# Two operations moved earlier and two moved later in the tail of an RWKV and mixture-of-experts kernel

## What is computed

```python
x = layernorm(x + attn(x))      # mixes, key/value/receptance products, a recurrence over tokens, product with Wo
x = layernorm(x + ffn(x))

def ffn(x):                     # E = 8 experts, K = 2 taken, I = 16
    weights = softmax(x @ router_w.T)
    gate    = weights * topk_mask(weights, 2)
    h       = einsum('bth,eih->beti', x, down_w)
    a       = silu(h)
    return sum over experts of gate * (a @ up_w)
```

## Time and profile before

| | us |
|---|---|
| median of 3 executions | 460.04 |
| lowest and highest | 459.71, 460.34 |
| the profiled execution, its own time | 459.98 |
| its span in the profile | 458.2 |
| TensorE busy in the span | 444.6 (97%) |
| VectorE busy | 404.1 (88%) |
| ScalarE busy | 356.0 (78%) |
| GpSimd busy | 312.0 (68%) |

### The profile page before, as it was taken

How to read it: one execution, slowest core, us unless ns; L and a number is a source line. 1 busy time by engine, 2 the same in 40 slices (tenths; PEclk the granted TensorE clock), 3 DMA queues, 4 the chain that set the end, 5 groups by cost and what they waited for, 6 DMA issues and landing times.

```text
span 458.2 us, 6679 instructions
## 1 busy us (share of the span) xinstructions
PE 444.6 (97%) x1984; PEld 340.2 (74%) x1984; DVE 404.1 (88%) x616; ACT 356.0 (78%) x801; POOL 312.0 (68%) x300
## 2 busy tenths in 40 slices
PE   8999999999999999999999999999999999999993
PEld 3444567777888888888888888888888888888761
DVE  5989989899788989999898998989898996876976
ACT  1666757877888779888788888888798887768695
POOL 2355677588658998579858797569966694744334
PEclk9999999999999999999999999999999999999998
DMA  8703230033000042002320042100520022300016
GB/s 239 223 0 117 93 92 1 1 115 93 1 1 0 2 160 92 24 0 74 135 70 0 1 139 93 46 0 24 162 93 1 1 69 94 137 1 0 0 49 229
DMA packets 20244, 30.64 MB, mean 67 GB/s; under 512 B 2032, under 2 KB 7152, under 8 KB 20208
## 3 DMA queue, kind: packets, MB, share of 16 engines
q1 hardware_dynamic: 20208, 30.21, 20.3%
HBM read 21.82 MB, written 8.39 MB: 66 GB/s over the span
## 4 chain that ended last, share of the span: by engine, by line
PE 78%; DVE 5%; ACT 2%; POOL 2%; issue 1%; ACTq 0%; DVEq 0%
PE PH L449 5%; PE PV L330 5%; PE PV L336 5%; PE PV L331 5%; PE PR L336 5%; PE PR L330 5%; PE PK L330 5%; PE PR L331 5%; PE PK L336 5%; PE PK L331 5%; PE PP L359 4%; PE PP L360 4%; PE PP L364 4%; PE PT L431 3%; PE PP L379 2%
## 5 line engine op out<-in xcount | busy, mean ns | idle before, releaser
L592 ACT ACTIVATE PR<-PR 128x512 f32<-128x512 f32 x128 | 74.6, 583 | 29.8 <-PE PR L336 10.6
L1213 POOL TENSOR_TENSOR DQ<-DEN,EX 128x512 f32<-128x512 f32 x32 | 41.3, 1290 | 20.6 <-DVE DEN L871 20.6
L1219 POOL TENSOR_SCALAR NM<-SUM,RS 128x1 f32<-128x1 f32 x30 | 8.0, 267 | 62.1 <-ACT RS L592 62.1
L330 PE MATMUL PK<-KH,WKH 128*128 128x512 f32 x112 | 46.2, 413 | 0.6 <-DVE NUM L888 0.6
L925 DVE SCALAR_TENSOR_TENSOR KT<-D,VEC,XT 128x512 f32<-128x512 f32 x57 | 45.8, 851 | 0.0
L330 PE MATMUL PV<-VH,WVH 128*128 128x512 f32 x112 | 45.6, 407 | 0.0
L336 PE MATMUL PR<-RL,WRH 128*128 128x512 f32 x112 | 44.0, 393 | 0.7 <-POOL RL L1181 0.7
L330 PE MATMUL PR<-RH,WRH 128*128 128x512 f32 x112 | 44.5, 398 | 0.2 <-DVE RW L912 0.2
L336 PE MATMUL PV<-VL,WVH 128*128 128x512 f32 x112 | 43.9, 392 | 0.0
L336 PE MATMUL PK<-KL,WKH 128*128 128x512 f32 x112 | 43.9, 392 | 0.0
L331 PE MATMUL PK<-KH,WKL 128*128 128x512 f32 x112 | 43.8, 391 | 0.0
(11 more groups left out here) (275 smaller groups left out, 1285.7 us busy)
## 6 DMA issues: line engine op xcount, KB each, us to landing
XT<-in_xt SPq DMA_DIRECT2D x32, 256.0 KB, 3.3
XN<-in_x SPq DMA_DIRECT2D x28, 256.0 KB, 2.7
out<-XN SPq DMA_DIRECT2D x28, 256.0 KB, 2.0
X1T<-in_wo SPq DMA_DIRECT2D x1, 1024.0 KB, 5.1
XT<-in_x SPq DMA_DIRECT2D x4, 256.0 KB, 4.2
out<-XT SPq DMA_DIRECT2D x4, 256.0 KB, 2.4
X1T<-in_wk SPq DMA_DIRECT2D x2, 256.0 KB, 4.9
XN<-in_wv SPq DMA_DIRECT2D x2, 256.0 KB, 5.7
```

What stands on the lines that cost most here:

```text
L330: eng.matmul(dst[:, :], wh[:, c, o], high[:, c, :], start=(c == 0), stop=False)
L592: eng.activation(*a, **k).then_inc(q[s], 1)
L1213: eng.tensor_tensor(DQ[:, :], DEN[:, 0:T], EX[:, 1, :], ALU.add).then_inc(q["e"], 1)
```

## The change

Three orders in the tail are altered. No instruction is added or taken away, and no wait is altered.

```diff
@@ TensorE @@
             hidden(t7 + 2)
+            hidden(t7 + 3)
             ffn_up(t5 + 3)
-            hidden(t7 + 3)
             ffn_up(t6)
@@ ScalarE @@
             hidden_copy(t7 + 2)
-            spread2(t5 + 1)
             hidden_copy(t7 + 3)
             ffn_in(LAST + 1)
             ffn_out(LAST)
+            spread2(t5 + 1)
             spread2(t5 + 2)
             ffn_out(LAST + 1)
@@ VectorE @@
             silu(LAST)
-            residual2(t5 + 3)
             gate_scores(LAST + 1)
             gate_top(LAST + 1)
+            residual2(t5 + 3)
             silu(LAST + 1)
```

## The result

| | before | after |
|---|---|---|
| median, same chip, 21 executions each (us) | 460.05 | 460.87 |
| the profiled execution, its own time | 459.98 | 460.70 |
| its span | 458.2 | 458.9 |

The changed kernel takes 0.82 us more; the ratio is 1.002, with a 95% interval from 1.0014 to 1.0025. The forecast was 460.8. Of all executions reported here one stands apart and is left out of its comparison: one of the eleven of e1 took 1162.12 us, and as it was the profiled one, the same kernel was profiled once more as e5, in a single execution of 461.21 us.

What follows compares the result with a forecast made beforehand. Taken to bound the tail: ScalarE's full queue from the last score copy, through GpSimd's scalings to the piled-up stores. TensorE 0, VectorE's 0.50 hidden beside ScalarE's 0.80: 459.98 + 0.80 = 460.78, median 460.8 us, range 460.2 to 461.4.

Steps and rivals of the forecast that it cites:

- Starts at 441.26 again: gain 0: TensorE: tile 31's reordered down product waits for ScalarE's copy of the transposed tile, so gains 0, at most 0.14 us.
- Hidden, just: TensorE: running tile 23's up product later costs at most 0.95 us, absorbed by the wait before part 8's transposes.
- 0.90 less a credit of 0.10: ScalarE: tile 21's squares, moved into the full queue, make it 0.90 us late, less 0.10: a shift of 0.80.
- The credit of 0.10: VectorE's subtraction for the last scores: 0.10 us shorter once GpSimd no longer scales tile 21 beside it; bounds 0 and 0.10.
- + 0.50: VectorE: tile 23's residual, exposed before the last two multiplications, delays them 0.60 less 0.10 us; bounds 0.46 and 0.60.
- Side by side, and the larger counts: Tail: VectorE's 0.50 us and ScalarE's 0.80 us delays run in parallel to the end; only the larger counts.
- a sign of being wrong: End of kernel: the last store is issued 0.8 us later but the end moves by less.
- 0.80 for the whole: Final stores: their transfers pile up; the pile begins 0.80 us later, so the whole kernel ends 0.80 later.
- No loss: Rival, chance 0.17: the store queue hides ScalarE's delay, or only VectorE's 0.50 us shows; 460.0 to 460.5 us.
- The stores bunch: Rival, chance 0.12: stores from tile 21's on run into each other, adding one tile of 0.75 us; 461.5 at worst.
- The clock: Rival, chance 0.02: TensorE's idle time halves its clock, adding 7.7 us on nine tiles' up products; some 468 us.
- A gain: Rival, chance 0.03: the last score copy comes earlier, by at most 0.14 and 0.10 us; 459.8 us.

Runs made afterwards that it cites:

- e1: Kernel before with only ScalarE's squares of tile 21 moved behind the copy of part 7: 460.91 us against 459.98, ratio 1.0021.
- e5: Same kernel as e1, profiled once more in a single execution: 461.21 us.
- e6: Changed kernel with ScalarE's copy of tile 31's transposed form put ahead of part 7's activations: 460.65 us against 460.05 for the kernel before, ratio 1.0015.
- e3: Kernel before with only tile 31's down product put ahead of tile 23's up product on TensorE: 460.87 us against 459.98, ratio 1.0021.
- e2: Kernel before with only VectorE's residual of tile 23 moved between the last gate and its two multiplications: 460.62 us against 459.98, ratio 1.0013.
- e4: Kernel before with the diffs of e2 and e3 together, without ScalarE's move: 460.56 us against 459.98, ratio 1.0012.
- e7: Kernel before with squares of tiles 22 and 23 taken as a pair ahead of part 8's copy on ScalarE: 459.70 us against 460.05, ratio 0.9993.
- e8: e7's pair, plus tile 27's up product ahead of part 8's transposes and tile 29's variance on ScalarE: 459.40 us against 460.05 before, ratio 0.9987.

## Why the prediction was right

**TensorE.** "Starts at 441.26 again: gain 0" held to 0.01, and e6 showed that its reason held: with the copy out of the way the product starts 0.85 earlier. "Hidden, just" was a bound from long steps; really TensorE reached the transposes of part 8 with 0.25 to spare. What the prediction left unsaid is that the move alone is not free. With the residual in its old place it costs 0.89 (e3).

**ScalarE.** 0.90 less a credit of 0.10 was right in the whole and in each part: two pitches of 1.09, the wait swallowed, the copy at 446.95 in after and in e5. That this queue carries the loss is shown by e5, where VectorE is early and the loss is all there.

**The credit of 0.10.** The subtraction takes 0.17 when GpSimd's scaling is not beside it (after, e5) and 0.27 when it is (before, e2), and then it ends 0.02 behind that scaling: 443.25 and 443.23 before, 443.56 and 443.54 in e2. The Trainium skill ("SBUF — State Buffer", section "SBUF: two separate sides") states that a VectorE operation with two SBUF inputs and a GpSimd operation that reads SBUF exclude each other for a whole instruction. These ends agree with it. The credit is most of the 0.12 between the 0.80 and the 0.92 of the prediction.

**VectorE.** + 0.50 was forecast, 0.48 measured in the changed kernel, 0.57 in e2 where the credit is missing (0.60 forecast as the upper bound). Behind the last multiplication stand eight residuals, tiles 24 to 31, and not the seven of the prediction; nothing in its sum used the count.

**The sum.** "Side by side, and the larger counts" is what e1, e2 and e4 say: 0.93, 0.64, 0.58, and 0.82 for all. The store of tile 31 missed its place, however: 455.80 was said, 455.87 + 0.08 = 455.95 came. GpSimd's scaling of tiles 28 and 30 took 1.92 and not the 1.68 of the earlier trace rows, and VectorE's of tiles 29 and 31 took 1.26 for 1.48. The prediction had carried both durations over, though their overlap moves with 0.50 against 0.80. The end did not follow the 0.15. The prediction had named as a sign of being wrong that the last store is issued 0.8 later and the end moves by less: the store moved by 0.95 and the end by 0.80, so the sign came half true, against the last tile and not against the pile. The table has what tells the two apart, in the profiled executions: how much later than before, the shift of each profile taken off, tile 26's store is issued (the pile's beginning), the last store is issued, and the whole execution ends.

| | tile 26's store | last store | end |
|---|---|---|---|
| after | 0.79 | 0.95 | 0.80 |
| e2 | 0.56 | 0.56 | 0.56 |
| e3 | 0.87 | 0.87 | 0.87 |
| e4 | 0.57 | 0.57 | 0.57 |
| e5 | 0.79 | 0.96 | 0.98 |
| e6 | 0.75 | 0.91 | 0.74 |
| e7 | -0.55 | -0.04 | -0.22 |
| e8 | -0.55 | -0.55 | -0.55 |

In six of eight the end follows the pile's beginning to 0.01, in after and e6 against the last store. The two others have a gap in the pile, which the DMA views of after and e6 do not have: tile 29's store in e7, as told, and in e5 the store of tile 28, whose scaling took 0.97 and not 0.77, with VectorE's of tile 29 beside it. So "0.80 for the whole" holds as long as no later store misses the pile. That none did in the changed kernel the prediction had not worked out; there it had some luck.

**The rivals.** *No loss*: falls with the result, and with e1 and e2. *The stores bunch*: in after the pile holds the same 1.57 MB, six tiles, as before, so tile 21's store didn't join it. *The clock*: 1.00 through the new idle time. (The "idle second" in the prediction is the one microsecond of the earlier trace rows.) *A gain*: the score copy came at 442.46 again.

## What to carry to other kernels

Before an operation is put ahead of another, read what it waits for: here its operand's copy stood behind five activations in another engine's queue, so going first gained nothing, and what it displaced was late. Work moved from beside a wait into a full queue costs its whole pitch, less only the waits that it swallows; follow each engine's queue separately to the end and take the larger delay, not the sum. Where two queues end close together, look at which work each of them still holds back when the other is shortened: e7, on one, gave 0.35 with an interval that reaches zero, and e8, on both, 0.65. Their intervals overlap, and no run shortened VectorE's alone.

## What was not expected

The scaling of a tile has no fixed price at the end. In e5 VectorE's two scalings of tiles 29 and 31, apart from each other, took 0.49 and 0.75 us; before they took 0.56 and 0.89. GpSimd's for the last two tiles together ranged from 1.52 (e7) to 1.92 (after). What differs is their place against VectorE's scalings; no run here isolates it as the cause. The last store and the end depend on it, as e5 shows above. VectorE in e5:

```profile
453.71 0.49 DVE L956 TENSOR_SCALAR XT<-XT,RS 128x512 f32<-128x512 f32 x1
454.37 0.75 DVE L956 TENSOR_SCALAR XT<-XT,RS 128x512 f32<-128x512 f32 x1 [0.17 <-ACT RS L666]
```
